# Conv 1's LayerNorm: squares with their row sums on ScalarE, reciprocal deviations by logarithm and exponential

## The chip, the cores and the metric

The kernel runs on one core of a Trainium2 chip. The metric is the device time of one execution in microseconds; the kernel before took 1780.17 us, the median of three runs (1779.33 to 1780.28).

The profile's names for the engines are PE (TensorE, matrix products and transposes), PEld (its weight loads), DVE (VectorE), ACT (ScalarE), POOL (GpSimd) and SP (SyncE, which starts transfers). Each engine takes its own instructions in order. Engines wait for each other through semaphores.

## The reference

A graph network over 50000 nodes of 64 channels and 25000 edges sorted by their target. In short, where `LN` is a LayerNorm over the 64 channels without weights:

```
h   = relu(LN(x))                                # x: 50000 x 64
h1  = relu(spline_conv(h,  src, dst, attr2, W1) )# conv 1
x   = x + spline_conv(h1, src, dst, attr2, W2)   # conv 2
x   = x + attention(relu(LN(x)), src, dst, attr3)
def spline_conv(x, ...):                         # K = 5 knots per axis, 25 matrices W
    msg = sum over 4 corners: basis * (x @ W[corner])[src]
    return segment_max(msg, dst) (0 where no edge) + x @ root + bias
```

The change is in the first line's LayerNorm: `(x - mean) / sqrt(var + 1e-5)` with `var = mean((x - mean)^2)`.

## The kernel before, in words

The edges are cut into 49 groups of 512 (four tiles of 128), the nodes into 49 groups of 1024 (128 partitions with 8 rows each). The program runs through a preparation, an MLP over the edge attributes, conv 1 (49 groups, about 108 to 640 us), a short pass of the MLP, conv 2, another pass, and the attention stage. Each engine's part of a stage is a function `step(g)` that is issued for every group, in a hardware loop whose body holds 12 groups of conv 1, with some groups before and behind it written out. The order of an engine's instructions is the order in which its `step` is written. No scheduler moves anything.

In conv 1, GpSimd gathers the rows of x for the sources of a group's edges, and SyncE loads the group's node rows. VectorE works on three groups in one step. For group g + 2 it does the statistics: sums of the rows (L1489 for the edges, 4 sums; L1493 for the nodes, 8 sums), the negative mean (L1503), and the centring of edge rows into `lnc` (L1509) and node rows into `nln` (L1514). For group g + 1 it multiplies the centred edge rows by the five knot weights of each tile, already multiplied by the reciprocal deviation (L1381 makes these weights `a0r`; L1410 is the spreading, `spread_z`, four per group). For group g it weighs TensorE's products (L1430, `weigh`, four per group), adds them up (L1438, L1444, L1451) and adds the bias to the node part (L1470). The running maximum along the edges is one scan per group (L1422). The node rows are multiplied by their reciprocal deviation in `node_in` (L1457).

TensorE turns the spread rows (L1020), multiplies them by the convolution's weights in two product pairs per group (L1027: the first for tiles 0 and 1, the second for tiles 2 and 3), turns messages (L1047), nodes (L1058) and results (L1095), and multiplies the nodes by the root matrix (L1069).

ScalarE evacuates the turned rows from PSUM with a ReLU (L797, four `evacuate` per group: tiles 2 and 3 of group g, then tiles 0 and 1 of group g + 1), copies the turned nodes (L835, `nhT`), the results (L852) and three small lists of numbers (L717, L807, L809). Between the evacuations of tiles 2 and 3 it squares the centred edge rows of group g + 2 (L827, one instruction of 128 x 256) and the centred node rows that belong to group g + 1 (L832, one of 128 x 512). VectorE then sums these squares (L1521, L1524), forms `sum / 64 + eps` for the 12 rows of a partition (L1531), ScalarE takes the square root (L843), and VectorE the reciprocal (L1541). The 12 sums, means, variances, roots and reciprocals of a step lie in the five rows of the tile `jst`.

Of the kernel before, what the change touches and what calls it, by code (L numbers as in the profile page):

```python
# [27 lines left out]
ALU = mybir.AluOpType  # L28
# [4 lines left out]
C = 64  # L33
# [90 lines left out]
def build(nc, a, out):  # L124
# [22 lines left out]
    with ExitStack() as ctx:  # L147
# [12 lines left out]
        def signals(prefix, names):  # L160

            return {n: steps(f"{prefix}_{n}", n) for n in names.split()}
# [229 lines left out]
        def conv_sems(n):  # L392
            s = {
                "nload": pair(f"c{n}_nload"), "nstore": pair(f"c{n}_nstore"), "cut": pair(f"c{n}_cut"),
                "z": steps(f"c{n}_z", "z0 z1 z2 z3"), "turn": steps(f"c{n}_turn", "t0 t1 t2 t3"), "prod": steps(f"c{n}_prod", "m0 m1 m2 m3"),
                "zt": steps(f"c{n}_zt", "zt0 zt1 zt2 zt3"), "comb": steps(f"c{n}_comb", "v0 v1 v2 v3 pair quad msg"),
                "npe": steps(f"c{n}_npe", "nt nr"), "out": steps(f"c{n}_out", "out" if n == 1 else "acc out"),
                **signals(f"c{n}", "mt agg at row xn nts"),
            }
            if n == 1:  # L400
                s.update(signals("c1", "gidx sidx rowid esum ecen esq evar nsum ncen nsq nvar root a0r"))
                s["gathered"], s["scattered"] = [sem(f"c1_gathered_{i}") for i in range(SLOTS)], [sem(f"c1_scattered_{i}") for i in range(SLOTS)]
                s["xstore"] = pair("c1_xstore")
                s["norm"] = steps("c1_norm", "mean eps rstd")
            else:
                s.update(signals("c2", "h idx et ets er"))
                s["gathered"] = [sem(f"c2_gathered_{i}") for i in range(SLOTS)]
                s["gidx"] = steps("c2_gidx", "src dst")
                s["base"] = steps("c2_base", "acc out")
                s["mstore"], s["tstore"], s["bstore"] = pair("c2_mstore"), pair("c2_tstore"), pair("c2_bstore")  # L410
            return s
# [282 lines left out]
        def _(act):  # L694
# [93 lines left out]
            def conv(n):  # L788
                s = cs[n]

                def step(g):
# [32 lines left out]
                    if n == 1 and (g + 2).within(G):  # L824
                        wait(act, s["ecen"], g + 2)
                        wait(act, s["evar"], g + 1)
                        act.activation(lnq[:, 0:TPG, :], lnc[:, half_of(g), :], ACT.Square)\  # L827
                            .then_inc(s["esq"].sem, 1)
                    if n == 1 and (g + 1).within(G):
                        wait(act, s["ncen"], g + 1)  # L830
                        wait(act, s["nvar"], g)
                        act.activation(nq[:, :, :], nln[:, :, :], ACT.Square).then_inc(s["nsq"].sem, 1)  # L832
# [8 lines left out]
                    if n == 1 and ((g + 1).within(G) or (g + 2).within(G)):  # L841
                        wait(act, s["norm"], g + 2, "eps")
                        act.activation(jst[:, 4, :], jst[:, 2, :], ACT.Sqrt).then_inc(s["root"].sem, 1)  # L843
# [17 lines left out]
            act.wait_ge(s_iota, 1)  # L861
            conv(1)
# [330 lines left out]
        def _(dve):  # L1193
# [179 lines left out]
            def conv(n):  # L1373
                s = cs[n]
                jsum, jmean, jv, jy, jt = (jst[:, k, :] for k in range(5))

                def scaled(g):

                    wait(dve, s["norm"], g, "rstd")
# [74 lines left out]
                def node_in(g):  # L1454
                    wait(dve, s["norm"], g + 1, "rstd")
# [29 lines left out]
                def sums(g):  # L1485
                    wait(dve, s["norm"], g - 1, "eps")
# [18 lines left out]
                def centre_rows(g):  # L1505
                    wait(dve, s["norm"], g, "mean")
                    if g.within(G):
                        wait(dve, s["z"], g - 2, "z3")
                        V_.tensor_tensor(lnc[:, half_of(g), :], xrows[g.slot(XS)],  # L1509
                                         jmean[:, 0:TPG].unsqueeze(2).broadcast_to([P, TPG, C]), ALU.add)\  # L1510
                            .then_inc(s["ecen"].sem, 1)
                    if (g - 1).within(G):
                        wait(dve, s["xn"], g - 2)
                        V_.tensor_tensor(nln[:, :, :], nx[1 - g.parity][:, :, 0:C],  # L1514
                                         jmean[:, TPG:].unsqueeze(2).broadcast_to([P, NPP, C]), ALU.add)\
                            .then_inc(s["ncen"].sem, 1)

                def variances(g):
                    if g.within(G):
                        wait(dve, s["esq"], g)  # L1520
                        V_.tensor_reduce(jsum[:, 0:TPG], lnq[:, 0:TPG, :], AX, ALU.add).then_inc(s["evar"].sem, 1)  # L1521
                    if (g - 1).within(G):
                        wait(dve, s["nsq"], g - 1)
                        V_.tensor_reduce(jsum[:, TPG:], nq[:, :, :], AX, ALU.add).then_inc(s["nvar"].sem, 1)  # L1524

                def plus_eps(g):
                    if g.within(G):
                        wait(dve, s["evar"], g)
                    if (g - 1).within(G):
                        wait(dve, s["nvar"], g - 1)  # L1530
                    V_.tensor_scalar(jv, jsum, 1.0 / C, EPS, ALU.mult, ALU.add).then_inc(s["norm"].sem, 1)  # L1531

                def step(g):
# [3 lines left out]

                    def roots():
                        if stats:
                            wait(dve, s["root"], e)  # L1540
                            V_.reciprocal(jy, jt).then_inc(s["norm"].sem, 1)  # L1541
# [25 lines left out]
                    if stats:  # L1567
                        variances(e)
                    if ahead:
                        spread_z(g + 1, 2)  # L1570
                    if stats:
                        plus_eps(e)
# [6 lines left out]
                    roots()  # L1579
# [139 lines left out]
```

## Time and profile before

| | |
|---|---|
| median of three runs | 1780.17 us (1779.33 to 1780.28) |
| the profiled execution's own time | 1782.96 us |
| its span, first to last instruction | 1781.2 us |
| TensorE busy | 1501.9 us (84%), 7834 matmuls |
| VectorE busy | 1399.4 us (79%), 2704 instructions |
| ScalarE busy | 740.8 us (42%), 1840 instructions |
| GpSimd busy | 1226.2 us (69%) |
| mean granted TensorE clock | 0.963 of full speed |

Busy times are sums over one profiled execution, averaged over stages that have different limits; the profile's table of stretches shows them stage by stage. The granted clock is 1.00 at 2.4 GHz and 0.50 at 1.2 GHz. In a timeline row the bracket at the end names how long the engine was idle before the instruction and what released it. Rows of a wait list read "who waited <- for whom: total us, times, longest".

### The profile page before, as it was taken

The page shows a single profiled execution, that of the slowest core. Times are in us where ns is not written, and L with a number is a line of the kernel's source. Part 1 is how long each engine was busy: PE and PEld are TensorE (multiplying, and loading weights), DVE is VectorE, ACT ScalarE, POOL GpSimd, SP SyncE. Part 2 cuts the span into 40 slices and gives each one's busy share as a digit, 9 for nine tenths or more (in the row PEclk, how much of TensorE's full clock was granted, in tenths as well). Part 3 has the DMA queues.
Part 4 walks back from the last instruction along what each step waited for, and adds up shares of the span by engine and source line. Part 5 has one row for each costly group of instructions (what it writes and reads, how often), then busy time and mean ns, then how long its engine had stood idle before and what let it go on. Part 6 is the DMA issues. An engine that isn't in the chain of part 4 may idle for free.

```text
span 1781.2 us, 33286 instructions
## 1 busy us (share of the span) xinstructions
PE 1501.9 (84%) x7834; PEld 1000.7 (56%) x7834; DVE 1399.4 (79%) x2704; ACT 740.8 (42%) x1840; POOL 1226.2 (69%) x1207
## 2 busy tenths in 40 slices
PE   3978888888889988999999999997777777677764
PEld 2856665665666655777777777775443333333332
DVE  6259999999999966888888888885676667666664
ACT  3533333333333353333333333335555545555553
POOL 6716777777774457777777777742577777777776
PEclk9989999999999988999999999997999989999997
DMA  8994444444443435877777887863333332323330
GB/s 133 177 129 101 103 102 102 102 106 99 107 104 91 97 75 157 211 207 208 207 205 202 203 204 205 204 179 92 73 70 73 74 68 72 69 69 69 69 75 19
DMA packets 451961, 218.67 MB, mean 123 GB/s; under 512 B 306089, under 2 KB 432058, under 8 KB 451896
## 3 DMA queue, kind: packets, MB, share of 16 engines
q1 hardware_dynamic: 355584, 138.37, 30.6%
q0 software_dynamic: 44864, 65.52, 17.4%
q10 hardware_dynamic: 51448, 14.14, 5.9%
q14 instruction: 51, 0.42, 0.1%
q8 instruction: 14, 0.23, 0.1%
HBM read 128.08 MB, written 92.64 MB: 124 GB/s over the span
## 4 chain that ended last, share of the span: by engine, by line
PE 33%; POOL 12%; issue 9%; ACT 4%; DMA 3%; DVE 3%; POOLq 0%; DVEq 0%; ACTq 0%; SPq 0%
PE bank L1027 18%; POOL gath L615 7%; POOL out_dram L622 6%; PE bank L1020 3%; PE bank L1069 2%; PE bank L1086 2%; DMA gath<-M,gidx 2%; PE bank L1151 2%; PE bank L1058 1%; PE bank L1047 1%; PE bank L1078 1%; PE bank L1095 1%; PE bank L1170 1%; DMA arena<-T 1%; DVE arena L1641 1%
## 5 line engine op out<-in xcount | busy, mean ns | idle before, releaser
L1027 PE MATMUL bank<-Wk,arena 128*128 128x320 f32 (+1 forms) x2352 | 655.4, 464 | 54.9 <-ACT arena L797 54.9
L1027 PEld LDWEIGHTS bank<-Wk,arena 128*128 128x128 f32 (+1 forms) x2352 | 327.0, 189 | 301.4 <-issue 223.6
L615 POOL DMA_INDIRECT gath<-T,gidx x392 | 393.6, 1004 | 132.7 <-issue 127.1
L622 POOL DMA_INDIRECT T<-srow,sidx x196 | 213.0, 1087 | 135.9 <-ACT srow L809 74.1
L797 ACT ACTIVATE arena<-bank 128x256 f32<-128x256 f32 (+1 forms) x392 | 168.8, 432 | 312.4 <-PE bank L1020 312.2
L615 POOL DMA_INDIRECT gath<-M,gidx x196 | 210.7, 1075 | 118.7 <-issue 55.5
L1430 DVE TENSOR_TENSOR arena<-bank,A 128x320 f32<-128x320 f32 x392 | 191.4, 488 | 84.5 <-PE bank L1027 80.3
L639 POOL DMA_INDIRECT gath<-in_x_dram,gidx x196 | 194.0, 990 | 87.2 <-issue 57.0
L622 POOL DMA_INDIRECT out_dram<-srow,sidx x196 | 199.1, 1016 | 61.4 <-issue 60.7
L1020 PE MATMUL bank<-ident,arena 128*128 128x128 f32 x980 | 171.8, 274 | 14.3 <-DVE arena L1410 14.3
L1020 PEld LDWEIGHTS bank<-ident,arena 128*128 128x128 f32 x980 | 124.0, 141 | 45.8 <-issue 12.2
L1422 DVE TENSOR_TENSOR_SCAN arena<-ends_cut,arena,bank 64x512 f32<-64x512 bf16 x98 | 123.6, 1261 | 0.9 <-PE bank L1047 0.9
L1170 PE MATMUL bank<-lnq,means 128*128 128x512 f32 x98 | 56.1, 654 | 75.7 <-ACT lnq L921 75.7
L1151 PE MATMUL bank<-arena,Wqk 128*128 128x512 f32 x98 | 60.8, 705 | 55.6 <-DVE arena L1629 55.6
L1069 PE MATMUL bank<-rootpair,nhT 128*128 128x128 f32 x784 | 103.5, 275 | 0.0
L1144 PE MATMUL bank<-DT,spread 128*128 (+1 forms) x392 | 102.6, 385 | 0.0
L1629 DVE SCALAR_TENSOR_TENSOR arena<-bank,arena 128x512 f32<-128x512 f32 x49 | 33.9, 692 | 85.8 <-ACT arena L928 85.8
L1069 PEld LDWEIGHTS bank<-rootpair,nhT 128*128 128x128 f32 x784 | 95.4, 192 | 0.3
L814 ACT ACTIVATE arena<-bank 128x512 f32<-128x512 f32 x49 | 29.3, 598 | 155.2 <-PE bank L1078 155.2
L1410 DVE TENSOR_TENSOR arena<-lnc,a0r 128x320 f32<-128x320 f32 x196 | 93.5, 479 | 0.0
L904 ACT ACTIVATE arena<-bank 128x512 f32<-128x512 f32 x49 | 29.3, 597 | 145.1 <-PE bank L1161 145.1
L1144 PEld LDWEIGHTS bank<-DT,spread 128*128 128x128 f32 x392 | 72.6, 196 | 29.4 <-issue 24.0
(212 smaller groups left out, 2669.8 us busy)
## 6 DMA issues: line engine op xcount, KB each, us to landing
T<-arena SPq DMA_DIRECT2D x96, 272.0 KB, 4.1
arena<-T SPq DMA_DIRECT2D x48, 544.0 KB
T<-zero ACTq DMA_DIRECT2D x1, 13281.2 KB, 104.3
B<-arena SPq DMA_DIRECT2D x49, 256.0 KB
arena<-B SPq DMA_DIRECT2D x49, 256.0 KB, 3.7
arena<-in_x_dram SPq DMA_DIRECT2D x48, 256.0 KB
out_dram<-arena SPq DMA_DIRECT2D x48, 256.0 KB
begins_cut<-begins_d SPq DMA_DIRECT2D x49, 128.5 KB, 3.5
```

What stands on the lines that cost most here:

```text
L615: pool.indirect_dma_start(out=gath[slot][:, j, k, 0:width], out_offset=None, in_=table, in_offset=bass.IndirectOffsetOnAxis(gidx[slot][:, ...
L622: pool.indirect_dma_start(out=table, out_offset=bass.IndirectOffsetOnAxis(sidx[g.slot(SLOTS)][:, j:j + 1], 0), in_=srow[g.slot(SLOTS)][:, ...
L639: pool.indirect_dma_start(out=xrows[slot][:, j, :], out_offset=None, in_=a["x"], in_offset=bass.IndirectOffsetOnAxis(xidx[slot][:, j:j + 1 ...
L797: act.activation(ZT[j // 2][:, first:first + chunks, :], bank[j % 2][:, 0:chunks * P], ACT.Relu)\
L1020: tr = pe.transpose(bank[j % 2][:, c * P:c * P + P], Z[g.parity][:, j // 2, (first + c) * P:(first + c + 1) * P], ident[:, :])
L1027: return pe.matmul(bank[2 + r][:, 0:KO], ZT[q][rows, chunk, :], Wk[n - 1][rows, weights].rearrange("p k o -> p (k o)"), start=start, stop= ...
L1069: mm = pe.matmul(bank[7][:, q * P:q * P + P], nhT[:, q * P:q * P + P], root[n - 1][:, :], start=True, stop=True)
L1144: pe.matmul(bank[b + e.parity].rearrange("p (t h e) -> p h t e", h=2, e=P)[:, j], spread[:, j, :], pairs, start=(j == 0), stop=False, skip ...
L1151: pe.matmul(bank[b + g.parity][:, :], W[:, :, :].rearrange("p t c -> p (t c)"), XT[g.parity][:, :], start=False, stop=True, skip_group_che ...
L1410: V_.tensor_tensor(Z[g.parity][:, j // 2, at_:at_ + KO].rearrange("p (k c) -> p k c", c=C), row.broadcast_to([P, K, C]), w.unsqueeze(2).br ...
L1422: V_.tensor_tensor_scan(agg[g.parity][:, ::-1], ends_cut[g.parity][:, ::-1], bank[4][0:C, ::-1], agg[1 - g.parity][:, 0:1], ALU.add, ALU.max)\
L1430: V_.tensor_tensor(V[:, j].rearrange("p (k o) -> p k o", o=C), bank[2 + j % 2][:, 0:KO].rearrange("p (k o) -> p k o", o=C), A1[:, bass.ds( ...
```

## The change

ScalarE's two squares become twelve, one for each tile row of 64 channels, and each of them also writes the sum of its 64 squares into one column of `jst` (`accum_out`). VectorE's two reductions of the squares, its scaling with epsilon and its reciprocal are removed. In their place ScalarE takes `ln(sum / 64 + eps)` and then `exp(-0.5 * that)`, behind the evacuation of tile 3 where the square root stood. The semaphores that told of variances, epsilon, root and reciprocal are replaced by one for `ln` and `exp`; VectorE's centring additionally waits for the squares of two groups before, and ScalarE's exponential for the users of the previous reciprocal deviations. A table load for logarithm and exponential is added ahead of conv 1. In the changed file ScalarE's lines move by up to 15 and VectorE's by 16, so L1430 becomes L1446.

```diff
@@ -398,10 +398,10 @@
                 **signals(f"c{n}", "mt agg at row xn nts"),
             }
             if n == 1:
-                s.update(signals("c1", "gidx sidx rowid esum ecen esq evar nsum ncen nsq nvar root a0r"))
+                s.update(signals("c1", "gidx sidx rowid esum ecen esq nsum ncen nsq a0r"))
                 s["gathered"], s["scattered"] = [sem(f"c1_gathered_{i}") for i in range(SLOTS)], [sem(f"c1_scattered_{i}") for i in range(SLOTS)]
                 s["xstore"] = pair("c1_xstore")
-                s["norm"] = steps("c1_norm", "mean eps rstd")
+                s["norm"], s["rstd"] = steps("c1_mean", "mean"), steps("c1_rstd", "ln exp")
             else:
                 s.update(signals("c2", "h idx et ets er"))
                 s["gathered"] = [sem(f"c2_gathered_{i}") for i in range(SLOTS)]
@@ -823,13 +823,18 @@
                             .then_inc(s["idx"].sem, 1)
                     if n == 1 and (g + 2).within(G):
                         wait(act, s["ecen"], g + 2)
-                        wait(act, s["evar"], g + 1)
-                        act.activation(lnq[:, 0:TPG, :], lnc[:, half_of(g), :], ACT.Square)\
-                            .then_inc(s["esq"].sem, 1)
+                        wait(act, s["rstd"], g + 1, "ln")
+                        for j in range(TPG):
+                            sq = act.activation(lnq[:, j, :], lnc[:, g.parity * TPG + j, :], ACT.Square,
+                                                accum_out=jst[:, 2, j:j + 1])
+                        sq.then_inc(s["esq"].sem, 1)
                     if n == 1 and (g + 1).within(G):
                         wait(act, s["ncen"], g + 1)
-                        wait(act, s["nvar"], g)
-                        act.activation(nq[:, :, :], nln[:, :, :], ACT.Square).then_inc(s["nsq"].sem, 1)
+                        wait(act, s["rstd"], g + 1, "ln")
+                        for j in range(NPP):
+                            sq = act.activation(nq[:, j, :], nln[:, j, :], ACT.Square,
+                                                accum_out=jst[:, 2, TPG + j:TPG + j + 1])
+                        sq.then_inc(s["nsq"].sem, 1)
                     if n == 1 and g.within(G):
                         wait(act, s["npe"], g, "nt")
                         act.activation(nhT[:, :], bank[6][:, :], ACT.Relu).then_inc(s["nts"].sem, 1)
@@ -839,8 +844,18 @@
                         wait(act, s["npe"], g, "nt")
                         act.activation(nhT[:, :], bank[6][:, :], ACT.Relu).then_inc(s["nts"].sem, 1)
                     if n == 1 and ((g + 1).within(G) or (g + 2).within(G)):
-                        wait(act, s["norm"], g + 2, "eps")
-                        act.activation(jst[:, 4, :], jst[:, 2, :], ACT.Sqrt).then_inc(s["root"].sem, 1)
+                        if (g + 2).within(G):
+                            wait(act, s["esq"], g + 2)
+                        if (g + 1).within(G):
+                            wait(act, s["nsq"], g + 1)
+                        wait(act, s["rstd"], g + 1, "exp")
+                        act.activation(jst[:, 4, :], jst[:, 2, :], ACT.Ln, scale=1.0 / C, bias=eps_col[:, :])\
+                            .then_inc(s["rstd"].sem, 1)
+                        wait(act, s["rstd"], g + 2, "ln")
+                        if (g + 1).within(G):
+                            wait(act, s["a0r"], g + 1)
+                        wait(act, s["xn"], g)
+                        act.activation(jst[:, 3, :], jst[:, 4, :], ACT.Exp, scale=-0.5).then_inc(s["rstd"].sem, 1)
                     if (g + 1).within(G):
                         evacuate(g + 1, 0)
                         evacuate(g + 1, 1)
@@ -859,6 +874,7 @@
             nc.scalar.mul(Wqk[C:P, :, :], Wqk[C:P, :, :], -1.0).then_inc(s_neg, 1)
 
             act.wait_ge(s_iota, 1)
+            act.preload_act_table_set("natural_log_exp_and_others")
             conv(1)
             for g in range(SLOTS):
                 wait_fill(act, cs[1]["gathered"], Group(None, G - SLOTS + g), 16 * TPG)
@@ -1372,11 +1388,11 @@
 
             def conv(n):
                 s = cs[n]
-                jsum, jmean, jv, jy, jt = (jst[:, k, :] for k in range(5))
+                jsum, jmean, jy = (jst[:, k, :] for k in (0, 1, 3))
 
                 def scaled(g):
 
-                    wait(dve, s["norm"], g, "rstd")
+                    wait(dve, s["rstd"], g, "exp")
                     wait(dve, s["z"], g - 1, "z3")
                     V_.tensor_tensor(a0r[:, :, :], back_tiles_of(A0, g),
                                      jy[:, 0:TPG].unsqueeze(2).broadcast_to([P, TPG, KR]), ALU.mult)\
@@ -1452,7 +1468,7 @@
                         .then_inc(s["comb"].sem, 1)
 
                 def node_in(g):
-                    wait(dve, s["norm"], g + 1, "rstd")
+                    wait(dve, s["rstd"], g + 1, "exp")
                     wait(dve, s["npe"], g - 1, "nt")
                     V_.tensor_tensor(nh[:, :, :], nln[:, :, :],
                                      jy[:, TPG:].unsqueeze(2).broadcast_to([P, NPP, C]), ALU.mult)\
@@ -1483,7 +1499,7 @@
                         .then_inc(s["base"].sem, 1)
 
                 def sums(g):
-                    wait(dve, s["norm"], g - 1, "eps")
+                    wait(dve, s["norm"], g - 1)
                     if g.within(G):
                         wait_fill(dve, s["gathered"], g, 16 * TPG)
                         V_.tensor_reduce(jsum[:, 0:TPG], xrows[g.slot(XS)], AX, ALU.add)\
@@ -1506,39 +1522,21 @@
                     wait(dve, s["norm"], g, "mean")
                     if g.within(G):
                         wait(dve, s["z"], g - 2, "z3")
+                        wait(dve, s["esq"], g - 2)
                         V_.tensor_tensor(lnc[:, half_of(g), :], xrows[g.slot(XS)],
                                          jmean[:, 0:TPG].unsqueeze(2).broadcast_to([P, TPG, C]), ALU.add)\
                             .then_inc(s["ecen"].sem, 1)
                     if (g - 1).within(G):
                         wait(dve, s["xn"], g - 2)
+                        wait(dve, s["nsq"], g - 2)
                         V_.tensor_tensor(nln[:, :, :], nx[1 - g.parity][:, :, 0:C],
                                          jmean[:, TPG:].unsqueeze(2).broadcast_to([P, NPP, C]), ALU.add)\
                             .then_inc(s["ncen"].sem, 1)
-
-                def variances(g):
-                    if g.within(G):
-                        wait(dve, s["esq"], g)
-                        V_.tensor_reduce(jsum[:, 0:TPG], lnq[:, 0:TPG, :], AX, ALU.add).then_inc(s["evar"].sem, 1)
-                    if (g - 1).within(G):
-                        wait(dve, s["nsq"], g - 1)
-                        V_.tensor_reduce(jsum[:, TPG:], nq[:, :, :], AX, ALU.add).then_inc(s["nvar"].sem, 1)
-
-                def plus_eps(g):
-                    if g.within(G):
-                        wait(dve, s["evar"], g)
-                    if (g - 1).within(G):
-                        wait(dve, s["nvar"], g - 1)
-                    V_.tensor_scalar(jv, jsum, 1.0 / C, EPS, ALU.mult, ALU.add).then_inc(s["norm"].sem, 1)
 
                 def step(g):
                     now, ahead = g.within(G), (g + 1).within(G)
                     e = g + 2
                     stats = n == 1 and (e.within(G) or ahead)
-
-                    def roots():
-                        if stats:
-                            wait(dve, s["root"], e)
-                            V_.reciprocal(jy, jt).then_inc(s["norm"].sem, 1)
 
                     if now and n == 1:
                         node_in(g)
@@ -1564,19 +1562,14 @@
                         scan(g - 1)
                     if now and n == 2:
                         base_out(g)
-                    if stats:
-                        variances(e)
                     if ahead:
                         spread_z(g + 1, 2)
-                    if stats:
-                        plus_eps(e)
                     if now:
                         weigh(g, 2)
                     if ahead:
                         spread_z(g + 1, 3)
                     if now:
                         weigh(g, 3)
-                    roots()
                     if now:
                         add_pairs(g)
                         add_quads(g)
```

ScalarE, in the loop's body, from the evacuation of tile 2 (`arena<-bank 128x256`) to that of tile 3 (`arena<-bank 128x384`) and what follows. ISA and REGISTER_ALU rows compute and await semaphore values. Before:

```order
L797 ACTIVATE arena<-bank 128x256
L114 ISA
L114 REGISTER_ALU
L827 ACTIVATE lnq<-lnc 128x256
L114 REGISTER_ALU
L832 ACTIVATE arena<-arena 128x512
L114 ISA
L835 ACTIVATE nhT<-bank 128x512
L114 REGISTER_ALU
L797 ACTIVATE arena<-bank 128x384
L114 ISA
L843 ACTIVATE jst<-jst 128x12
```

The same place in the changed kernel:

```order
L797 ACTIVATE arena<-bank 128x256
L114 ISA x2
L828 ACTIVATE lnq,jst<-lnc 128x64 x4
L114 REGISTER_ALU
L835 ACTIVATE arena,jst<-arena 128x64 x8
L114 REGISTER_ALU
L840 ACTIVATE nhT<-bank 128x512
L114 REGISTER_ALU
L797 ACTIVATE arena<-bank 128x384
L114 REGISTER_ALU
L852 ACTIVATE jst<-jst,eps_col 128x12
```

Twelve squares stand where two stood, ahead of the copy to `nhT` and of tile 3's evacuation; the logarithm stands where the square root stood, and the exponential follows it.

VectorE, in the loop's body, from the second weighing of a group to its last one. Before:

```order
L1430 TENSOR_TENSOR arena<-bank,A 128x320
L1422 SCALAR_TENSOR_TENSOR arena<-ends_cut,arena,bank 64x512
L1521 TENSOR_REDUCE jst<-lnq 128x4
L1524 TENSOR_REDUCE jst<-arena 128x8
L1410 TENSOR_TENSOR arena<-lnc,a0r 128x320
L1531 TENSOR_SCALAR jst<-jst 128x12
L114 REGISTER_ALU
L1430 ISA
L1430 TENSOR_TENSOR arena<-bank,A 128x320
L1410 TENSOR_TENSOR arena<-lnc,a0r 128x320
```

The same place in the changed kernel:

```order
L1446 TENSOR_TENSOR arena<-bank,A 128x320
L1438 SCALAR_TENSOR_TENSOR arena<-ends_cut,arena,bank 64x512
L1426 TENSOR_TENSOR arena<-lnc,a0r 128x320
L114 REGISTER_ALU
L1446 ISA
L1446 TENSOR_TENSOR arena<-bank,A 128x320
L1426 TENSOR_TENSOR arena<-lnc,a0r 128x320
```

Three instructions are gone between the scan and the third weighing (the reciprocal, a few rows later, too). What stands between a group's first weighing and the centring is the same in both.

## Rows read from the trace of the kernel before

**Rows 1.** Windows: stretch, length, PE, PEld, DVE, ACT, POOL busy (count), PEclk, DMA, GB/s.
```profile
108.00:640.00 532.00, 469.63 (x2592) 320.29 (x2593) 503.09 (x1169) 190.22 (x570) 348.99 (x332) 0.99 0.46 100
...
1230.00:1781.00 551.00, 387.40 (x1407) 207.49 (x1405) 368.13 (x551) 286.97 (x604) 409.84 (x392) 0.93 0.31 68
```

**Rows 2.** Timeline of VectorE, node scaling L1457: start, length, engine, line.
```profile
130.24 0.68 DVE L1457 TENSOR_TENSOR arena<-arena,jst 128x512 f32<-128x512 f32 x1
...
640.45 0.68 DVE L1457 TENSOR_TENSOR arena<-arena,jst 128x512 f32<-128x512 f32 x1
```

**Rows 3.** Waits of 180 to 600 us: total, times, longest.
```profile
PE bank L1027 <- ACT arena L797: 43.3, 38, 1.6
...
DVE arena L1430 <- PE bank L1027: 9.2, 37, 0.3
...
ACT arena L832 <- DVE arena L1514: 7.0, 38, 0.2
```

**Rows 4.** Timeline of ScalarE, one round in conv 1.
```profile
593.31 0.48 ACT L797 ACTIVATE arena<-bank 128x384 f32<-128x384 f32 x1
...
597.93 0.20 ACT L807 ACTIVATE sidx<-thirdI 128x4 int32<-128x4 int32 x1
598.03 0.20 ACT L809 ACTIVATE srow<-rowI 128x4 f32<-128x4 int32 x1
...
602.33 0.42 ACT L827 ACTIVATE lnq<-lnc 128x256 f32<-128x256 f32 x1 [0.79 <-DVE lnc L1509]
602.93 0.63 ACT L832 ACTIVATE arena<-arena 128x512 f32<-128x512 f32 x1 [0.18 <-DVE arena L1514]
603.47 0.58 ACT L835 ACTIVATE nhT<-bank 128x512 f32<-128x512 f32 x1
603.94 0.48 ACT L797 ACTIVATE arena<-bank 128x384 f32<-128x384 f32 x1
605.90 0.21 ACT L843 ACTIVATE jst<-jst 128x12 f32<-128x12 f32 x1 [1.47 <-DVE jst L1531]
```

**Rows 5.** Timeline of TensorE in the same round.
```profile
593.92 2.08 PE L1027 MATMUL bank<-Wk,arena 64*128 64x320 f32 x8 [0.92 <-ACT arena L797]
...
597.55 3.36 PE L1027 MATMUL bank<-Wk,arena 128*128 128x320 f32 x12
```

**Rows 6.** Timeline of VectorE in the same round.
```profile
599.66 0.49 DVE L1430 TENSOR_TENSOR arena<-bank,A 128x320 f32<-128x320 f32 x1 [0.17 <-PE bank L1027]
```

**Rows 7.** Groups by line on VectorE, 180 to 600 us: busy, mean ns.
```profile
L1524 DVE TENSOR_REDUCE jst<-arena 128x8 f32<-128x512 f32 x38 | 25.3, 666 | 0.0
...
L1521 DVE TENSOR_REDUCE jst<-lnq 128x4 f32<-128x256 f32 x38 | 14.5, 383 | 0.0
...
L1541 DVE RECIPROCAL jst<-jst 128x12 f32<-128x12 f32 x39 | 8.5, 217 | 0.0
...
L1531 DVE TENSOR_SCALAR jst<-jst 128x12 f32<-128x12 f32 x39 | 6.1, 155 | 0.0
```

**Rows 8.** Groups by line and form on ScalarE, 180 to 600 us.
```profile
L832 ACT ACTIVATE arena<-arena 128x512 f32<-128x512 f32 x38 | 23.9, 630 | 7.0 <-DVE arena L1514 7.0
...
L827 ACT ACTIVATE lnq<-lnc 128x256 f32<-128x256 f32 x38 | 15.8, 417 | 41.0 <-DVE lnc L1509 41.0
```

**Rows 9.** Timeline of ScalarE before conv 1.
```profile
104.94 1.28 ACT L769 ACT_TABLE_LOAD   x1
...
109.78 0.42 ACT L827 ACTIVATE lnq<-lnc 128x256 f32<-128x256 f32 x1 [2.14 <-DVE lnc L1509]
```

**Rows 10.** Windows of two short stretches; columns as in Rows 1.
```profile
117.00:121.00 4.00, 4.00 (x9) 1.88 (x10) 0.89 (x3) 0.18 (x2) 2.38 (x3) 0.50 1.02 178
...
1358.00:1363.00 5.00, 4.41 (x9) 1.89 (x8) 1.25 (x3) 1.70 (x5) 3.78 (x5) 0.50 0.64 101
```

**Rows 11.** Timeline of TensorE: conv 1's beginning, and the last stage.
```profile
116.76 5.71 PE L1027 MATMUL bank<-Wk,arena 128*128 128x320 f32 x12 [2.40 <-ACT arena L797]
...
1356.35 1.10 PE L1170 MATMUL bank<-lnq,means 128*128 128x512 f32 x2 [1.97 <-ACT lnq L921]
```

## The prediction

> **What bounds the kernel now.** I read the stages first. In each stretch of the table of windows the reader is to see the busy times beside the granted clock: conv 1 (108 to 640 us) keeps VectorE busy 503.09 of 532 us and TensorE 469.63, at a granted clock of 0.99; the last stage (1230 to 1781 us) keeps TensorE busy 387.40 of 551 us at 0.93 [rows 1]. Only conv 1 has edited instructions in its loop. Its 49 groups give a line 1457 each; from the second (130.24) to the last (640.45) are 47 periods of 10.86 us [rows 2]. VectorE's share per group is 503.09 / 49 = 10.27 us, so it looks like the bound. It isn't quite: three waits recur in nearly every group, and they close a ring [rows 3]. The second product's matmuls (L1027) wait 43.3 us in 38 groups for ScalarE's evacuation L797; VectorE's first weighing (L1430) waits 9.2 us, 37 times, for TensorE; ScalarE's node square (L832) waits 7.0 us, 38 times, for VectorE's centring L1514.
>
> One round of that ring, late in conv 1:
> - ScalarE's last evacuation of the group starts at 593.31 and ends at 593.79 [rows 4]. TensorE, idle 0.92 us for it, starts the second product at 593.92 and the next group's first product at 597.55 [rows 5]. VectorE, idle 0.17 us for that product, weighs its first tile at 599.66 [rows 6]. TensorE's part of the ring: 599.66 - 593.79 = 5.87 us.
> - VectorE then takes sums, spreads and means in its order and centres the edge rows; ScalarE starts their square at 602.33 [rows 4]. VectorE's part: 2.67 us.
> - ScalarE squares edges, waits 0.18 us for L1514, squares nodes, copies nhT from 603.47 and evacuates from 603.94 to 604.42 [rows 4]. Its part: 2.09 us, of which 1.14 us lie between the first square's start and nhT's start.
> Sum 5.87 + 2.67 + 2.09 = 10.63 us, the round from 593.79 to 604.42. The ring sets the period; the 0.17 us is all that VectorE has to spare at its turn.
>
> **What is taken away.** Per group VectorE loses the two reductions of squares (0.666 and 0.383), the scaling with epsilon (0.155) and the reciprocal (0.217): 1.42 us [rows 7]. All of them stand on VectorE between the scan and the next group's start. None lies in the 2.67 us between the first weighing and the centring, so none is on the ring. VectorE comes earlier to its first weighing and waits there longer for TensorE. I cost this gain at nothing; what would hide it is the 5.87 us of TensorE. ScalarE's square root goes too; it was issued behind the last evacuation, off the ring.
>
> **What is added on the ring.** Two squares (0.417 us for 256 columns, 0.630 for 512 [rows 8]) become twelve of 64 columns, each with a sum that is written out. By the two rows a column costs (0.630 - 0.417) / 256 = 0.00083 us, so a 64-column square is 0.417 - 192 x 0.00083 = 0.257 us long. Neighbours overlap: the copies at 597.93 and 598.03 last 0.20 and start 0.10 apart, and nhT starts 0.09 before the node square ends [rows 4]. Without any cost of the sum, squares would follow each other every 0.257 - 0.10 = 0.16 us: that is the lower bound. The trace has no ScalarE instruction that writes a sum. If the sum is read out by something like another small ACTIVATE, its nearest rows are those copies: 0.10 us if it is pipelined behind its square (0.26 each), 0.20 more and no overlap at all if each waits for the one before (0.46 each), the upper bound. I take the middle of 0.26 and 0.36 (read-out after the square has ended, next square overlapping it), 0.31 us; I keep 0.16 and 0.46 for the range.
>
> The Trainium skill says in "VectorE: DVE Perf Modes", section "Two Vector instructions with no wait between them", that an operation which also writes out its accumulator is two instructions there, the main one and an accumulator read. That speaks of VectorE, and no row here shows it for ScalarE; if it holds there too, the price would be some pair as above and not the 0.16.
>
> The piece of 1.14 us becomes 12 x 0.31 = 3.72 us. What is queued behind the squares on ScalarE is nhT and the evacuation that TensorE already waits for. So each group grows by 3.72 - 1.14 = 2.58 us, to 13.44, and 47 periods by 121 us (at 0.16: 0.78 and 37; at 0.46: 4.38 and 206). The node squares' wait of 0.18 us for L1514 vanishes under the four edge squares; that is in the difference.
>
> **The rest.** The logarithm and exponential follow the last evacuation, where ScalarE stands idle from 604.42 to 605.90 for VectorE's scaling and then takes the square root [rows 4]; two small ACTIVATEs with a wait between are some 0.5 us (from the 0.20 us copies), and TensorE's first product, which needs the next evacuations, starts 3.76 us after the last one's end [rows 4, 5]. Cost nothing; if the cover went, 0.5 us a group, 24 us. The waits of the exponential for nodes and a0r of this step are met some 5 us earlier. On VectorE the centring's new waits for squares of two groups before are met long since. The extra table load (1.28 us) falls before conv 1, where ScalarE next waits 2.14 us for the first centring [rows 9]: at most nothing to 1 us. The two steps before the first group have squares of the same kind with nothing beside them: about 1 us more. DMA issues don't move.
>
> **The clock.** TensorE's idle piece per group grows from 0.92 to 3.5 us. In the last stage the clock was granted at 0.50 after an idle piece of 1.97 us [rows 10, 11], and its mean of 0.93 [rows 1] is 14% of the time at the lower level, with TensorE busy 70%. Conv 1 would come to 9.58 (469.63 / 49) of 13.44 us, 71%. At the lower level twelve matmuls took 5.71 us [rows 11] against 3.36 [rows 5]: 0.41 us lost per us. 14% of 13.44 us is 1.88 us, worth 0.77 us if all of it lies in TensorE's part of the ring and 0.34 if spread evenly; the middle, 0.55 us, over 47 groups is 26 us.
>
> **The sum.** 121 + 1 + 26 = 148 us on the profiled execution's 1782.96, which lies 2.8 us above the median of the runs; on the median 1780.17 that is 1928, rounded to 1930 us.
>
> **Rivals.**
> - The sum costs nothing: pitch 0.16, 37 us more, 1817. For: each square is a single ACTIVATE in the program's order. Against: a sum per row has to leave the engine somehow, and every written result in this trace has its fixed time. By the Trainium skill, "ScalarE: Activation LUTs", section "What ACT_TABLE_LOAD costs", an ACTIVATE takes 186 ns plus 0.833 ns a column and overlaps its neighbour by 93 ns; the rows agree with both, and a plain square would follow after 146 ns, for 1809 us (an estimate from that page). Chance 0.12.
> - The clock falls in every round, since the idle piece is now longer than any that recurs in the last stage: 2.35 us more per group (the twelve matmuls' loss), (2.58 + 2.35) x 47 = 232, so 2012 us. For: the row after 1.97 us of idleness. Against: a mean of 0.93 in a stage with such pieces in most groups. Chance 0.12.
> - Faster: twelve short squares stream with their fixed parts wholly overlapped, 64 x 0.00083 = 0.053 us each, 0.64 us instead of 1.14; the ring shrinks by 0.50 us, 24 us in all, 1757. It decides at a pitch of 0.095 us. For: small copies already hide half of their length. Against: none starts closer than 0.10 behind another. Chance 0.03.
> - VectorE is the bound after all, and the ring has slack that I don't see: the 1.42 us then count against the growth, and it decides at a pitch of (1.14 + 1.42) / 12 = 0.21 us. At 0.16 a group shrinks by 0.64 us, 30 us in all, 1750; at 0.26 it grows by 0.56 us, 1806. For: VectorE is busy 95% of conv 1 [rows 1]. Against: its 37 waits for TensorE [rows 3]. Chance 0.05.
>
> **Numbers.** The forecast has 0.68. Pitches of 0.26 to 0.36 with 0 to 50 us of clock give 1875 to 1985 for it alone. The range takes in the sum at nothing on one side, and on the other the pitch of 0.46 (1780 + 206 + 1 = 1987) with some 60 us for the clock: 1815 to 2050. Two tenths of a per cent (3.6 us) is what a measurement of this kernel can tell from no change. Faster: 0.03 from the short squares and 0.02 from VectorE as the bound, 0.05; same: 0.02, of the last rival near the pitch at which it decides; slower: the rest, 0.93.
>
> **What would show it.** The period of VectorE's node scaling near 13.4 us; TensorE's second product waiting 3 us or more for the evacuation in every group; squares every 0.31 us, with or without rows of their own for the sum; VectorE's wait at the first weighing up from 0.2 us to 4; the granted clock in conv 1 below 0.99. Wrong if the squares follow each other in under 0.16 us, if VectorE still has no wait at its first weighing, or if the period grows while TensorE doesn't wait for ScalarE.

## The result and the profile after

The changed kernel takes 1953.33 us (median of 4 runs, 1949.25 to 1955.63) against 1780.22 us of the kernel before beside it: 1.0968 times as long, 95% interval 1.0947 to 1.0990. The profiled execution took 1952.18 us, its span is 1950.4 us.

The table of stretches, in the columns of [rows 1], has conv 1 at 108 to 830 us and the last stage at 1400 to 1950 us.

```profile
108.00:830.00 722.00, 571.40 (x2662) 383.42 (x2662) 465.60 (x984) 302.37 (x1722) 355.27 (x344) 0.85 0.34 75
...
1400.00:1950.00 550.00, 389.00 (x1408) 208.89 (x1407) 368.10 (x552) 287.36 (x604) 409.02 (x392) 0.92 0.32 68
```

The last stage is as it was. Conv 1 has grown, VectorE is busy for less time in it (465.60 against 503.09 us [rows 1]), and TensorE's clock fell from a mean of 0.99 to 0.85. VectorE's node scaling, now line 1473, shows the period as [rows 2] did:

```profile
133.07 0.68 DVE L1473 TENSOR_TENSOR arena<-arena,jst 128x512 f32<-128x512 f32 x1
...
811.04 0.68 DVE L1473 TENSOR_TENSOR arena<-arena,jst 128x512 f32<-128x512 f32 x1
```

677.97 / 47 = 14.43 us, 3.57 more than the 10.86 before; 47 x 3.57 = 168 of the 173 us. The waits of 180 to 600 us, against [rows 3]:

```profile
DVE arena L1446 <- PE bank L1043: 140.8, 85, 3.0
...
PE bank L1043 <- ACT arena L797: 84.1, 29, 3.3
```

TensorE waits for tile 3's evacuation 84.1 / 29 = 2.90 us in each group, where it waited 43.3 / 38 = 1.14. VectorE, which lost rows of 1.42 us per group, now waits 140.8 / 29 = 4.86 us per group for TensorE's products. The timeline of ScalarE in one round answers to [rows 4]:

```profile
602.51 0.26 ACT L828 ACTIVATE lnq<-lnc 128x64 f32<-128x64 f32 x1 [0.98 <-DVE lnc L1526]
602.68 0.19 ACT L828 ACTIVATION_READ_ACCUMULATOR lnq<-lnc 128x1 f32 x1
602.77 0.24 ACT L828 ACTIVATE lnq<-lnc 128x64 f32<-128x64 f32 x1
602.92 0.18 ACT L828 ACTIVATION_READ_ACCUMULATOR lnq<-lnc 128x1 f32 x1
...
605.15 0.24 ACT L835 ACTIVATE arena<-arena 128x64 f32<-128x64 f32 x1
605.30 0.18 ACT L835 ACTIVATION_READ_ACCUMULATOR arena<-arena 128x1 f32 x1
605.39 0.57 ACT L840 ACTIVATE nhT<-bank 128x512 f32<-128x512 f32 x1
605.87 0.47 ACT L797 ACTIVATE arena<-bank 128x384 f32<-128x384 f32 x1
606.24 0.29 ACT L852 ACTIVATE jst<-jst,eps_col 128x12 f32<-128x12 f32 x1
```

Each sum is an instruction of its own, ACTIVATION_READ_ACCUMULATOR, which the program's order doesn't show. It overlaps the square before it and the square after it, so squares follow each other every 0.24 us (602.77 and, for the last of the twelve, 605.15: ten steps in 2.38 us). From the first square to nhT are 605.39 - 602.51 = 2.88 us, 1.14 before.

TensorE's timeline in the same round, against [rows 5], and three windows in it (columns of [rows 1]):

```profile
602.37 1.24 PE L1043 MATMUL bank<-Wk,arena 128*128 128x320 f32 x4
606.47 3.87 PE L1043 MATMUL bank<-Wk,arena 64*128 64x320 f32 x8 [2.85 <-ACT arena L797]
...
610.77 1.92 PE L1085 MATMUL bank<-rootpair,nhT 128*128 128x128 f32 x8
...
613.04 3.36 PE L1043 MATMUL bank<-Wk,arena 128*128 128x320 f32 x12
```

```profile
603.00:606.00 3.00, 0.61 (x3) 0.10 (x1) 2.04 (x4) 3.00 (x24) 2.30 (x3) 0.98 0.34 84
607.00:610.00 3.00, 3.00 (x8) 1.40 (x5) 0.89 (x2) 0.05 (x1) 2.15 (x3) 0.50 0.60 118
613.00:616.00 3.00, 3.00 (x14) 1.69 (x13) 1.76 (x5) 0.67 (x4) 1.21 (x2) 1.00 0.37 84
```

After 2.85 us of idleness the clock is at its lower level: the eight matmuls behind the wait take 3.87 us instead of 2.08 [rows 5]. By 613 it is back, and the first product takes its 3.36 us again. This isn't an odd round. In all 45 rounds of conv 1 whose timeline shows these eight matmuls whole, they take 2.51 to 3.87 us, except in the last. The next round's and the last round's:

```profile
621.97 3.02 PE L1043 MATMUL bank<-Wk,arena 64*128 64x320 f32 x8 [2.85 <-ACT arena L797]
...
806.27 2.08 PE L1043 MATMUL bank<-Wk,arena 64*128 64x320 f32 x8 [1.56 <-ACT arena L797]
```

The growth of a round is therefore two things: squares ahead of the evacuation, and slower matmuls behind it.

### The profile page after: what moved, and what is told of

Read it like the earlier page. It is cut to its first block, busy times and chain, and to the rows that moved or that the text cites. A ratio compares the mean times of both kernels' runs of the same rounds, so it can differ in the third digit from the quotient of the medians.

```text
span 1950.4 us, 34215 instructions
## 1 busy us (share of the span) xinstructions
PE 1590.2 (82%) x7834; PEld 1055.2 (54%) x7834; DVE 1354.2 (69%) x2506; ACT 846.0 (43%) x2969; POOL 1220.0 (63%) x1207
## 4 chain that ended last, share of the span: by engine, by line
PE 31%; POOL 10%; issue 8%; ACT 4%; DMA 3%; DVE 3%; POOLq 0%; DVEq 0%; ACTq 0%; SPq 0%
PE bank L1043 16%; POOL gath L615 6%; POOL out_dram L622 4%; PE bank L1036 3%; PE bank L1085 2%; PE bank L1102 2%; PE bank L1167 2%; DMA gath<-M,gidx 2%; PE bank L1074 1%; PE bank L1063 1%; PE bank L1094 1%; PE bank L1186 1%; PE bank L1111 1%; DVE arena L1634 1%; DMA arena<-T 1%
## 5 line engine op out<-in xcount | busy, mean ns | idle before, releaser
L1043 PE MATMUL bank<-Wk,arena 128*128 128x320 f32 (+1 forms) x2352 | 718.3, 500 | 138.2 <-ACT arena L797 138.2
L1043 PEld LDWEIGHTS bank<-Wk,arena 128*128 128x128 f32 (+1 forms) x2352 | 351.2, 202 | 405.4 <-issue 327.2
L622 POOL DMA_INDIRECT T<-srow,sidx x196 | 205.8, 1050 | 311.9 <-ACT srow L809 253.2
L1446 DVE TENSOR_TENSOR arena<-bank,A 128x320 f32<-128x320 f32 x392 | 191.9, 490 | 293.5 <-PE bank L1043 293.5
L797 ACT ACTIVATE arena<-bank 128x256 f32<-128x256 f32 (+1 forms) x392 | 168.1, 431 | 442.5 <-PE bank L1036 442.4
L1036 PE MATMUL bank<-ident,arena 128*128 128x128 f32 x980 | 183.7, 290 | 15.2 <-DVE arena L1426 15.2
L1036 PEld LDWEIGHTS bank<-ident,arena 128*128 128x128 f32 x980 | 135.1, 152 | 58.9 <-issue 33.7
L1085 PE MATMUL bank<-rootpair,nhT 128*128 128x128 f32 x784 | 119.0, 302 | 0.0
L1085 PEld LDWEIGHTS bank<-rootpair,nhT 128*128 128x128 f32 x784 | 113.1, 222 | 0.3
L835 ACT ACTIVATE arena<-arena 128x64 f32<-128x64 f32 x392 | 93.5, 239 | 0.7 <-DVE arena L1532 0.7
```

What stands on the lines that cost most here:

```text
L622: pool.indirect_dma_start(out=table, out_offset=bass.IndirectOffsetOnAxis(sidx[g.slot(SLOTS)][:, j:j + 1], 0), in_=srow[g.slot(SLOTS)][:, ...
L797: act.activation(ZT[j // 2][:, first:first + chunks, :], bank[j % 2][:, 0:chunks * P], ACT.Relu)\
L835: sq = act.activation(nq[:, j, :], nln[:, j, :], ACT.Square, accum_out=jst[:, 2, TPG + j:TPG + j + 1])
L1036: tr = pe.transpose(bank[j % 2][:, c * P:c * P + P], Z[g.parity][:, j // 2, (first + c) * P:(first + c + 1) * P], ident[:, :])
L1043: return pe.matmul(bank[2 + r][:, 0:KO], ZT[q][rows, chunk, :], Wk[n - 1][rows, weights].rearrange("p k o -> p (k o)"), start=start, stop= ...
L1085: mm = pe.matmul(bank[7][:, q * P:q * P + P], nhT[:, q * P:q * P + P], root[n - 1][:, :], start=True, stop=True)
```

## The experiments

All runs were timed beside the kernel before, which took 1781.5 to 1782.1 us (medians) in these sets.

**Two whole squares, no sums.** The changed kernel's squares made whole again, the variances left out altogether.

```diff
-for j in range(TPG):
-    sq = act.activation(lnq[:, j, :], lnc[:, ...], ACT.Square, accum_out=jst[:, 2, j:j + 1])
-sq.then_inc(s["esq"].sem, 1)
+act.activation(lnq[:, 0:TPG, :], lnc[:, half_of(g), :], ACT.Square).then_inc(s["esq"].sem, 1)
 ...  # nodes alike
```

> The changed kernel with its two squares whole again (128x256 and 128x512) and without any sum of them: the variances are left out of the computation, VectorE has none of the removed work back. The ring theory (the period is set by evacuation, products, first weighing, centring, squares, evacuation, and nothing that VectorE lost lies on it) expects the period of before, 10.86 us, and 1780 us within 8. The rival, that VectorE's 1.42 us per group counted, expects some 1.2 us less per group, 1720 us.

Measured: 1781.16 us, ratio 1.0005 (0.9994 to 1.0015). VectorE has all four instructions taken away and nothing is won. Its waits of 180 to 600 us for the products show where that time went, while TensorE's wait for the evacuation stayed (43.3 us in [rows 3]):

```profile
DVE arena L1441 <- PE bank L1038: 48.4, 113, 0.7
PE bank L1038 <- ACT arena L797: 43.1, 38, 1.5
```

Before, VectorE waited 9.2 us for them [rows 3], so (48.4 - 9.2) / 38 = 1.03 us per group are new. That is what was really taken away: the four rows add up to 1.42 us, but rows on VectorE overlap their neighbours (late in conv 1 of the kernel before, the first reduction starts at 604.41 us and lasts 0.38, and the second starts at 604.72). The windows of 180 to 600 us, in the kernel before and in this one, have VectorE busy for 399.38 - 362.55 = 36.83 us less, 0.95 us per group:

```profile
180.00:600.00 420.00, 374.23 (x2081) 255.65 (x2080) 399.38 (x925) 150.99 (x455) 298.36 (x284) 1.00 0.46 102
180.00:600.00 420.00, 373.76 (x2078) 255.19 (x2077) 362.55 (x771) 157.54 (x491) 300.96 (x286) 1.00 0.47 102
```

All of it turned into waiting. The ring sets the period; the rival that VectorE was the bound falls.

**Logarithm and exponential alone.** Two whole squares, VectorE's two reductions as before, and the new roots:

```diff
-V_.tensor_scalar(jv, jsum, 1.0 / C, EPS, ALU.mult, ALU.add)      # VectorE
-act.activation(jst[:, 4, :], jst[:, 2, :], ACT.Sqrt)             # ScalarE
-V_.reciprocal(jy, jt)                                            # VectorE
+act.activation(jst[:, 4, :], jst[:, 2, :], ACT.Ln, scale=1.0 / C, bias=eps_col[:, :])
+act.activation(jst[:, 3, :], jst[:, 4, :], ACT.Exp, scale=-0.5)
```

> The other half of the change alone: two whole squares and VectorE's two reductions as before, but logarithm and exponential on ScalarE in place of VectorE's scaling with epsilon, the square root and the reciprocal. The ring theory expects no change, 1780 us within 5, since both stand behind the last evacuation and 3.8 us ahead of the first product. If the pair delays the next two evacuations enough, 0.5 us a group, 1804 us.

Measured: 1779.73 us, ratio 0.9989 (0.9979 to 0.9999): 2 us less, with an interval that ends just short of no change, and no loss. This half of the change costs nothing; the table load ahead of conv 1 is included.

**Twelve squares, no sums.** The loops of the change without `accum_out`.

```diff
-sq = act.activation(lnq[:, j, :], lnc[:, g.parity * TPG + j, :], ACT.Square, accum_out=jst[:, 2, j:j + 1])
+sq = act.activation(lnq[:, j, :], lnc[:, g.parity * TPG + j, :], ACT.Square)
```

> The changed kernel with its twelve squares but without their sums (the variances are left out of the computation). A square should follow the one before after 0.15 us instead of 0.24: 12 x 0.15 - 1.14 = 0.66 us more per group than before, 31 us. The ring theory expects 1811 us, and up to 1835 if the lower clock comes already at an idle piece of 1.6 us. If the cost were in the split and not in the sums, it would stay near 1950.

Measured: 1843.31 us, ratio 1.0339 (1.0319 to 1.0360), 8 us above the expected range. ScalarE's timeline (equal instructions merged):

```profile
507.91 0.69 ACT L828 ACTIVATE lnq<-lnc 128x64 f32<-128x64 f32 x4 [0.98 <-DVE lnc L1524]
508.51 1.28 ACT L834 ACTIVATE arena<-arena 128x64 f32<-128x64 f32 x8
509.70 0.57 ACT L838 ACTIVATE nhT<-bank 128x512 f32<-128x512 f32 x1
```

Twelve squares take 1.79 us, 0.15 each as expected, 0.65 more than before: 47 x 0.65 = 31 us. That leaves 31 us of 62 for the clock, of which I had allowed 24 at most; this share is a difference, and no run with a filler takes it apart here. In conv 1 of this run the clock's mean is 0.92:

```profile
108.00:735.00 627.00, 524.08 (x2698) 358.10 (x2698) 471.46 (x992) 261.02 (x1152) 370.32 (x352) 0.92 0.45 92
```

TensorE's timeline has two rounds with the same idle piece:

```profile
510.78 2.08 PE L1041 MATMUL bank<-Wk,arena 64*128 64x320 f32 x8 [1.77 <-ACT arena L797]
...
522.23 3.06 PE L1041 MATMUL bank<-Wk,arena 64*128 64x320 f32 x8 [1.76 <-ACT arena L797]
```

The second is one with a fall (3.06 us for eight matmuls), the first is not. Of the 46 rounds that the timeline shows whole, 20 have such a fall (2.42 to 3.73 us), behind pieces of 1.76 to 2.16 us; 15 others with pieces of 1.76 to 1.94 us have none, nor have the eight late ones with pieces of 1.56 to 1.58. So pieces of 1.8 us bring the clock down in some rounds, and the length of one piece alone doesn't decide in which.

**A filler that keeps the clock.** The changed kernel with transposes that nobody reads, in TensorE's idle piece:

```diff
 part(0, 1, 1, whole, False, False)
+if n == 1 and q == 1:
+    for _ in range(16):
+        pe.transpose(bank[5][:, 2 * P:3 * P], ident[:, :], ident[:, :])
 wait(pe, s["zt"], g, f"zt{2 * q + 1}")
```

> The changed kernel with 16 more transposes of the identity on TensorE in conv 1, per group, ahead of its wait for the last evacuation, into unused columns; they fill some 1.8 of the idle 2.85 us and nothing reads them. If about half of the growth is the lower clock, the granted clock in conv 1 goes back to about 1.00 and the period to 10.86 + 1.74 = 12.6 us: 1862 us, up to 1880 where the filler gets in the way. If the whole growth of 3.6 us per group is ScalarE's queue, nothing is gained: 1953 us or more.

Measured: 1866.43 us, ratio 1.0477 (1.0459 to 1.0494). TensorE in one round, and the window of 180 to 600 us:

```profile
504.40 1.91 PE L1053 MATMUL bank<-ident 128*128 128x128 f32 x16
507.42 2.08 PE L1043 MATMUL bank<-Wk,arena 64*128 64x320 f32 x8 [1.10 <-ACT arena L797]
```

```profile
180.00:600.00 420.00, 379.60 (x2316) 279.52 (x2314) 311.81 (x663) 200.41 (x1157) 283.06 (x264) 1.00 0.42 89
```

More work on TensorE makes the kernel 1953.33 - 1866.43 = 87 us shorter: the clock is granted in full, and the eight matmuls take 2.08 us again. That is the clock's share of the change. What is left, 1866 - 1782 = 84 us, is ScalarE's queue, for which 47 x (2.88 - 1.14) = 82 us were to be expected.

**The evacuation ahead of the squares.** In the kernel before, in the changed kernel, and in the one with logarithm and exponential alone, ScalarE evacuates tile 3 and copies nhT first:

```diff
+evacuate(g, 3)
+act.activation(nhT[:, :], bank[6][:, :], ACT.Relu).then_inc(s["nts"].sem, 1)
 act.activation(lnq[...], lnc[...], ACT.Square)      # edge squares, then node squares
 ...
-act.activation(nhT[:, :], bank[6][:, :], ACT.Relu).then_inc(s["nts"].sem, 1)
-evacuate(g, 3)
```

The kernel before with this order:

> The kernel before with tile 3's evacuation and the copy to nhT ahead of the two squares on ScalarE in conv 1. If the squares hurt only because the evacuation is queued behind them, the ring opens: TensorE no longer waits for the evacuation, and VectorE's own work of 10.27 us per group with its gaps sets the period, some 10.4 us: 47 x 0.45 = 21 us less, 1760 us. The rival, that the evacuation must be late because tile 3 is turned late, expects no change, 1780.

Measured: 1759.89 us, ratio 0.9877 (0.9860 to 0.9893), as expected. By the starts of node scaling most groups take 10.26 us, VectorE's 10.27.

The changed kernel with this order:

> The changed kernel with the same move: evacuation and nhT ahead of the twelve squares. The squares' 2.88 us then lie beside TensorE's second product; VectorE has 8.9 us of work per group, TensorE 9.6, and no idle piece that lowers the clock. By the ring theory TensorE sets the period, 9.6 to 9.9 us: 45 to 59 us less than before, about 1730. If the squares with their sums are too long for any place on ScalarE (then the next group's first two evacuations come late, by up to 1 us), 1770 to 1830.

Measured: 1751.45 us, ratio 0.9830 (0.9813 to 0.9846): the fastest complete version, and the same twelve squares that cost 173 us in their old place. TensorE's products wait for an evacuation only twice more in conv 1, and most groups take 9.63 us, TensorE's 9.6. But it isn't the 1730 us that I expected, and the squares aren't the reason: seven groups, those at the loop's seams aside, take 11.1 to 13.9 us, together 21 us more than seven of 9.63.

The third:

> Logarithm and exponential with two whole squares and VectorE's reductions, and evacuation and nhT first. VectorE has 10.27 - 0.155 - 0.217 = 9.9 us per group and sets the period: 10.0 to 10.1 us, 1740 to 1748. If TensorE's 9.6 us and not VectorE's work is what both reorderings end on, it equals the changed kernel with the evacuation first.

Measured: 1758.02 us, ratio 0.9867 (0.9850 to 0.9883), 10 us above the expected range and level with the first. Most groups take 10.17 us against 10.26 there. The two rows taken from VectorE were again worth less than their lengths: with logarithm and exponential alone it is busy 393.74 of the 420 us from 180 to 600, against 399.38 before, 0.15 us less per group and not 0.37:

```profile
180.00:600.00 420.00, 374.49 (x2082) 255.76 (x2081) 393.74 (x847) 161.78 (x492) 300.60 (x285) 1.00 0.48 102
```

So VectorE has some 10.1 us of work per group here, and it may well be what most groups end on in both versions; no run settles that. The rest lies in long groups, two of 13.5 and 13.6 us here against one of 13.4 in the first.

What the long groups are is seen in the changed kernel with the evacuation first. ScalarE waits there in 20 groups, up to 6.1 us, to refill a scatter's list of rows, for the scatter that used it. Where that wait is 4.8 us or longer, which is so in seven groups, its evacuation L797 comes late, and TensorE waits. The rows of the waits of 180 to 580 us, and one such group:

```profile
ACT sidx L807 <- DMA T<-srow,sidx: 67.1, 20, 6.1
PE bank L1036 <- ACT arena L797: 15.1, 7, 2.6
```

```profile
483.23 0.68 DVE L1473 TENSOR_TENSOR arena<-arena,jst 128x512 f32<-128x512 f32 x1
488.51 0.21 ACT L807 ACTIVATE sidx<-thirdI 128x4 int32<-128x4 int32 x1 [5.97 <-DMA T<-srow,sidx]
489.23 0.41 PE L1036 MATMUL bank<-ident,arena 128*128 128x128 f32 x2 [2.50 <-ACT arena L797]
497.17 0.68 DVE L1473 TENSOR_TENSOR arena<-arena,jst 128x512 f32<-128x512 f32 x1
```

GpSimd's groups by line in the same stretch show why the scatters are late:

```profile
L622 POOL DMA_INDIRECT T<-srow,sidx x157 | 170.7, 1087 | 54.9 <-issue 48.9 <-ACT srow L809 5.4 <-DVE lnc L1526 0.6
L639 POOL DMA_INDIRECT gath<-in_x_dram,gidx x131 | 136.2, 1039 | 39.9 <-issue 38.7 <-ACT srow L809 1.2
```

Busy 170.7 + 136.2 and issuing 48.9 + 38.7 us are 394.5 of 400 us: GpSimd has hardly a gap. 394.5 / 288 is 1.37 us for an indirect DMA, so the eight of a group take some 11 us (an estimate from these rows), longer than a group of 9.63 us. GpSimd falls behind, and from 335 us on ScalarE waits for it. In the kernel before, the same sum is already 374.4 of 400 us.

**Three scatters.** To test that, one scatter of the four is left out in conv 1, and with it tile 3's messages:

```diff
-for j in range(TPG):
+for j in range(TPG if s is not cs[1] else TPG - 1):
     pool.indirect_dma_start(out=table, ...)
```

> The changed kernel with the evacuation first, and in conv 1 only three of the four scatters of a group's messages (those of tile 3 are left out of the computation). If GpSimd's eight indirect DMAs of 1.3 us each set the period of 10.36 us there, seven of them take 9.1 us, and TensorE's 9.6 us are next: a period of 9.6 to 9.8 us, 26 to 35 us less than with four, 1716 to 1726 us. If ScalarE's squares or VectorE hold the period, nothing is gained: 1751 us within 4.

Measured: 1731.65 us, ratio 0.9726 (0.9704 to 0.9747), 20 us less than with four and 6 us above the expected range. ScalarE no longer waits for a scatter in any group, and the seven long groups are gone. So GpSimd's scatters made them, and lightening GpSimd gains. Other than the expectation has it, they didn't set the period of every group: most took 9.63 us with four scatters and take 9.64 with three. TensorE is then busy nearly all of 180 to 570 us:

```profile
180.00:570.00 390.00, 385.69 (x2158) 264.73 (x2156) 371.17 (x799) 244.19 (x1390) 268.96 (x249) 1.00 0.52 111
```

The mean period is 9.75 us, within the 9.6 to 9.8 expected. The 6 us come from the other end: the expectation set out from a period of 10.36 us with four scatters, and the starts of node scaling give 10.19 there, 47 x 0.17 = 8 us less to gain.

## Why the prediction was right

The direction and its reason held: squares lengthen the ring, and VectorE's lost work gives nothing back. The two sizes in the sum did not hold. One was too high and the other too low, so it is luck that the forecast of 1930 came within 24 us of the measured 1953.

- **The ring.** Right. Taking VectorE's four instructions away changed nothing (ratio 1.0005), and taking the squares out of the ring made even the changed kernel faster than before. The round of 10.63 us in the prediction is a late one; most earlier rounds take 10.82, and two 13.2.
- **VectorE's lost work.** Worth nothing, as forecast, but two readings were off. The rows of 1.42 us kept VectorE busy for 0.95 us only, since they overlap. And the prediction has VectorE wait longer at its first weighing. Without the four instructions that wait stays at 0.3 us, and the third and fourth weighing, ahead of which the work stood, wait 0.64 and 0.40 (means over conv 1).
- **The squares' price.** Too high. I put 0.31 us on a square with its sum; it is 0.24. The bounds 0.16 and 0.46 held. The read-out is an instruction with a row of 0.18 to 0.19 us, but it overlaps both its neighbours and adds only 0.24 - 0.15 = 0.09 us. The Trainium skill ("VectorE: DVE Perf Modes", section "Two Vector instructions with no wait between them") says of VectorE that an operation with an accumulator output is two instructions; this trace shows the same on ScalarE. The term was 121 us; it measures 82 by the rows and 84 by the run with the filler.
- **The clock.** Far too low: the term was 26 us, it measures 87. I took the last stage's share of time at the lower level, 14%, because TensorE's busy share would be equal there. That step was wrong: the mean of 0.85 in conv 1 is (1 - 0.85) / 0.5 = 30% of the time, 4.3 us of a round of 14.43. The idle time of a round is in one piece here, 2.85 us, and the lost time lies just behind that piece, where the ring is TensorE's own. At the prediction's 0.41 us lost per us, 4.3 us cost 1.8, and 87 / 47 = 1.85 us were measured. The rival with a fall in every round had the mechanism, since the clock fell in every whole round but the last; only its price of 2.35 us was too high. With the squares at their true price it gives the better sum: 82 + 87 = 169 us.
- **The sum.** 121 + 1 + 26 = 148 against 82 + 87 = 169 of the 173 measured. With the right pitch and my clock it would have been 1780 + 109 = 1889, with the right clock and my pitch 1989.
- **Logarithm and exponential, table load** were put at nothing to 1 us; measured at 2 us less to none.
- **What would show it.** The period near 13.4 was 14.4; TensorE's wait of 3 us or more was 2.90 on average. VectorE's new wait I had put at the first weighing. It lies mostly at the third: over conv 1 the first weighing waits 0.76 us on average, the third 2.69, the fourth 1.43. In the round shown the third and fourth waited 3.01 and 1.56 us, the first of the next round 1.24, since the whole second product comes late and not only what follows it:

```profile
608.05 0.49 DVE L1446 TENSOR_TENSOR arena<-bank,A 128x320 f32<-128x320 f32 x1 [3.01 <-PE bank L1043]
...
610.49 0.49 DVE L1446 TENSOR_TENSOR arena<-bank,A 128x320 f32<-128x320 f32 x1 [1.56 <-PE bank L1043]
...
615.36 0.49 DVE L1446 TENSOR_TENSOR arena<-bank,A 128x320 f32<-128x320 f32 x1 [1.24 <-PE bank L1043]
```

## What to carry to other kernels

An engine that is busy 95% of a stage need not be its bound: look for the short waits that recur once per round, follow them from engine to engine, and if they close, only work on that ring counts until it opens and the next bound shows. Rows of an engine can overlap, so what their removal frees is less than the sum of their lengths; read it from the busy time of a window. Work that is moved to an idle engine is free only if nothing urgent is queued behind it; here the order of two pieces on ScalarE decided between 173 us lost and 31 us gained. Where a ring grows by an idle piece on TensorE, price the clock behind that piece as well, and from rounds that have such a piece: here the mean of another stage with a like busy share gave 26 us, and 87 were measured.

## What the runs showed of the hardware

- ScalarE's sum output is a second instruction of 0.18 to 0.19 us that overlaps both neighbours: 64-column squares follow each other every 0.24 us with it and every 0.15 without.
- TensorE's matmuls ran slower behind idle pieces of 1.76 to 2.16 us in 20 of 46 rounds, and behind the changed kernel's pieces, mostly of 2.85 us, in every whole round but the last, at 1.85 us per round; from 607 to 610 us the granted clock was 0.50. Pieces of 1.10 us, with the filler, left the mean at 1.00.
- Sixteen useless transposes per group made the changed kernel 87 us faster.
- GpSimd's indirect DMAs took 1.04 to 1.09 us each with some 0.30 us of issue before the next; 288 of them left 5.5 of 400 us free.
- Instructions that added up to 1.42 us in the rows of VectorE's timeline freed 0.95 us of its busy time when they were removed.
